# Four transformer layers on one core: inputs in pieces, and another order at four places

## What is computed

```python
x = inputs                                             # (1, 2048, 128)
x = layernorm(x + attention(x, Wq, Wk, Wv, Wo, ...))   # 16 heads of 8, all keys
x = layernorm(x + rope_attention_and_top2_experts(x))  # causal, 16 heads; then 2 of 8 experts
x = layernorm(x + mamba2_block(x))                     # conv, state-space scan, then a gated MLP of 344
x = layernorm(x + experts16(x))                        # sigmoid scores, 8 of 16 experts, and a shared one

def experts16(x):
    scores = sigmoid(x @ gate.T); inds = top8(scores + bias)
    combine = onehot(inds) * 2.826 * scores[inds] / sum(scores[inds])
    y = sum_e combine[e] * (silu(x @ w_gate[e].T) * (x @ w_up[e].T)) @ w_down[e].T
    return y + (silu(x @ sg.T) * (x @ su.T)) @ sd.T
```

## Time and profile before

| | us |
|---|---|
| median of 3 runs | 1793.71 (1791.2 to 1806.1) |
| the profiled execution | 1793.51 |
| its span | 1791.7 |
| mean granted clock of PE | 0.97 |

### The profile page before, as it was taken

One profiled execution on the slowest core, in us unless ns is written; L12 is line 12 of the kernel. 1 busy time (PEld: TensorE's weight loads), 2 busy tenths in 40 slices (PEclk: granted clock), 3 DMA queues, 4 the chain that ended last, 5 costly groups with the idle time before them and its releaser, 6 DMA issues. The chain is left out here.

```text
span 1791.7 us, 25880 instructions
## 1 busy us (share of the span) xinstructions
PE 1662.0 (93%) x9970; PEld 781.1 (44%) x9970; DVE 1271.6 (71%) x1818; ACT 1192.6 (67%) x2434; POOL 199.3 (11%) x187
## 2 busy tenths in 40 slices
PE   6999999999999999879899999999878599799997
PEld 3433333333333333244344444455555266444443
DVE  4888888888888888257888677675376376555555
ACT  4578888888888888855677777777635656233432
POOL 1100000000000000041000000111244100001100
PEclk9899999999999999989999999999989799899999
DMA  1000000000000000010000000000000100302220
...
DMA packets 8330, 29.98 MB, mean 17 GB/s; under 512 B 712, under 2 KB 3152, under 8 KB 6032
## 3 DMA queue, kind: packets, MB, share of 16 engines
...
## 5 line engine op out<-in xcount | busy, mean ns | idle before, releaser
L911 DVE TENSOR_REDUCE a_part_max<-a_ps 128x2 f32<-128x1024 f32 x512 | 602.8, 1221 | 90.8 <-PE a_ps L714 90.2
L896 ACT ACTIVATE a_probs<-a_ps 128x512 f32<-128x512 f32 x1024 | 533.0, 613 | 131.0 <-PE a_ps L809 128.6
L911 DVE TENSOR_REDUCE f_part_max<-f_ps 128x2 f32<-128x1024 f32 (+3 forms) x320 | 328.2, 1062 | 127.4 <-PE f_ps L714 67.2
L809 PE MATMUL a_ps<-a_q_shift,a_KA 64*128 64x512 f32 x1024 | 367.4, 447 | 3.8 <-POOL a_q_shift L693 2.4
L896 ACT ACTIVATE f_probs<-f_ps 128x512 f32<-128x512 f32 (+3 forms) x640 | 300.3, 538 | 101.0 <-PE f_ps L809 49.2
L809 PEld LDWEIGHTS a_ps<-a_q_shift,a_KA 64*128 64x128 f32 x1024 | 166.4, 186 | 290.2 <-ACT a_probs L896 274.9
L714 PE MATMUL a_ps<-a_KA,a_q_open 64*128 64x512 f32 x1024 | 276.5, 467 | 4.9 <-DVE a_part_max L911 4.2
L829 PE MATMUL a_psO<-a_probs,a_VA 128*32 128x512 f32 x2048 | 274.7, 608 | 3.9 <-ACT a_probs L896 3.9
L809 PE MATMUL f_ps<-f_q_shift,f_KA 64*128 64x512 f32 (+3 forms) x640 | 223.4, 434 | 5.2 <-POOL f_q_shift L693 2.2
L714 PE MATMUL f_ps<-f_KA,f_q_open 64*128 64x512 f32 (+3 forms) x640 | 168.7, 427 | 7.1 <-DVE f_part_max L911 6.3
L809 PEld LDWEIGHTS f_ps<-f_q_shift,f_KA 64*128 64x128 f32 x640 | 105.8, 187 | 149.7 <-ACT f_probs L896 138.8
...
## 6 DMA issues: line engine op xcount, KB each, us to landing
...
```

The lines of the kernel that those rows point to most:

```text
L809: mm = pe.matmul(bank(r)[:, lo:512], g.KA[rows, 2 * n + jp, P * s:P * s + P], q_shift[rows, u % 2, jp, lo:512], start=True, stop=not diag)
L896: nc.scalar.activation(probs[:, st % 2, j, lo:512], bank(r)[:, lo:512], ACT.Exp, scale=SCALE).then_inc(ring_read, 1)
L911: dve.tensor_reduce(part_max[:, 4 * q + 2 * jp:4 * q + 2 * jp + 2, c], ps1[:, k % 2, :, 0:b - a], AX_X, ALU.max).then_inc(max_read, 1)
```

## The change

- `load_stage` is gone. The first attention's `front_stage` gets a `Loads` object and issues ten transfers in its own program: x in four blocks, the identity apart from the other constants, and the weights for q and k apart from the others. Each wait is for its own piece. The casts and fills come at the end of the front's ScalarE list, the three bf16 casts behind a wait for the last pieces.
- In the first step of both attentions, PE has scores 0, 1 and 2 ahead of the maxima of the first half.
- In the scan, `gate_up`, `gated`, `project_down`, `add_mlp` and `mean` stand earlier.
- In the experts, the shared expert's `products` of block 0 stand ahead of `turn_c`.
- The last block's scaling: two tiles on ScalarE, two on DVE.

```diff
+class Loads:
+    def __init__(self, g):
+        self.x = [g.sem("x_in%d" % b) for b in range(NB)]
+        self.ident, self.first, self.cols, self.rest = (g.sem("loaded_" + x) for x in ("ident", "first", "cols", "rest"))
+    def issue(self, sp, g):
+        aps = g.aps
+        tokens = aps["x"].rearrange("(t p) e -> p t e", p=P)
+        a, b = W_COLS["wq"][0], W_COLS["wk"][1]
+        def x_block(n):
+            sp.dma_start(g.X[:, 4 * n:4 * n + 4, :], tokens[:, 4 * n:4 * n + 4, :]).then_inc(self.x[n], 16)
+        x_block(0)
+        sp.dma_start(g.K[:, 0:P], aps["consts"][:, 0:P]).then_inc(self.ident, 16)
+        sp.dma_start(g.W[:, a:b], aps["weights"][:, a:b]).then_inc(self.first, 16)
+        x_block(1)
+        sp.dma_start(g.C[:], aps["cols"]).then_inc(self.cols, 16)
+        x_block(2)
+        x_block(3)
+        sp.dma_start(g.K[:, P:K_N], aps["consts"][:, P:K_N]).then_inc(self.rest, 16)
+        sp.dma_start(g.R[:], aps["rows"].partition_broadcast(P)).then_inc(self.rest, 16)
+        sp.dma_start(g.W[:, b:W_LATER], aps["weights"][:, b:W_LATER]).then_inc(self.rest, 16)
+        sp.wait_ge(self.rest, 48)
...
+                if loads:
+                    loads.issue(sp, g)
...
+                if loads:
+                    pool.memset(g.half[:], -0.5).then_inc(half_in, 1)
+                    pool.memset(g.q_spread[:].bitcast(F32), 0.0).then_inc(sel_clear, 1)
                 pool.memset(g.k_spread[:].bitcast(F32), 0.0).then_inc(sel_clear, 1)
                 pool.memset(g.VA[:], 1.0).then_inc(v_ones, 1)
...
+                    if loads:
+                        pe.wait_ge(loads.x[b], 16)
+                        if b == 0:
+                            pe.wait_ge(loads.ident, 16)
...
+                    if loads:
+                        pe.wait_ge(loads.first, 16)
                     pe.matmul(bank, g.w(wk if kind == "k" else wq), source[:, cols(b)], start=True, stop=True).then_inc(qk_ps, 1)
...
+                    if loads:
+                        act.wait_ge(loads.cols, 16)
...
-                    act.wait_ge(sel_clear, 1)
+                    act.wait_ge(sel_clear, 2)
+                    fill_spread(g, g.q_spread, Q_PARTS, sel_in)
                     fill_spread(g, g.k_spread, K_PARTS, sel_in)
+                    nc.scalar.copy(g.ident_r[:], g.k("ident")).then_inc(sel_in, 1)
+                    act.wait_ge(loads.rest, 48)
+                    for name, dst in (("ident_h", g.ident_h), ("mask_qk_h", g.mask_qk), ("mask_kq_h", g.mask_kq)):
+                        nc.scalar.copy(dst[:].rearrange("p h i -> p (h i)"), g.k(name)).then_inc(sel_in, 1)
...
                 more(plan.before)
                 for st in range(plan.first[-1]):
                     scores(st, 0)
-                    more(plan.halves[2 * st])
+                    if st:
+                        more(plan.halves[2 * st])
                     scores(st, 1)
                     scores(st, 2)
+                    if st == 0:
+                        more(plan.halves[0])
                     if st:
                         sums(st - 1)
                     scores(st, 3)
...
                     n = b + 1
                     for i in range(4):
                         c = 4 * b + i
+                        if c == 13:
+                            t.gate_up(pe, 0, 1, ring(0), ring(1))
...
                         if c == 12:
                             pe.wait_ge(ring_read, ITEMS * NB)
-                        if 12 <= c < 15:
-                            t.gate_up(pe, 0, c - 12, ring(0), ring(1))
+                            t.gate_up(pe, 0, 0, ring(0), ring(1))
                         outputs(c)
+                        if c == 13:
+                            t.gate_up(pe, 0, 2, ring(0), ring(1))
+                        if c == 14:
+                            t.project_down(pe, 0, ring(0))
...
-                t.project_down(pe, 0, ring(0))
...
                         if c + 1 < C:
                             carry_on(c)
+                        if c == 14:
+                            t.gated(dve, 0, 2, ring(1))
+                        if c == 15:
+                            t.add_mlp(dve, 0, ring(0), eps)
...
                         if c == 11:
                             t.scale(dve, 0)
-                        if c >= 13:
-                            t.gated(dve, 0, c - 13, ring(1))
+                        if c in (12, 13):
+                            t.gated(dve, 0, c - 12, ring(1))
+                        if c == 15:
+                            t.mean(dve, 0)
...
                 finish(C - 1)
-                t.add_mlp(dve, 0, ring(0), eps)
-                t.mean(dve, 0)
...
                 turn_x(0)
                 route(0)
+                products(0, 0)
                 turn_c(0)
                 for b in range(NB):
                     c = b + 1
                     for x in range(NX + 1):
-                        if x < NX:
+                        if x < NX and (b or x):
                             products(b, x)
...
                 def apply_out(b):
                     act.wait_ge(nb2, b + 1)
-                    apply_norm(nc, blk(g.X, b), blk(g.Y, b), rstd[:, 1, b, :], nb[:, 1, b, :], sent)
+                    n = 2 if b == NB - 1 else 4
+                    for i in range(4 * b, 4 * b + n):
+                        nc.scalar.activation(g.X[:, i, :], g.Y[:, i, :], ACT.Identity, scale=rstd[:, 1, b, i % 4:i % 4 + 1],
+                                             bias=nb[:, 1, b, i % 4:i % 4 + 1]).then_inc(sent, 1)
...
                 mean_out(NB - 1)
+                dve.wait_ge(nb2, NB)
+                for i in (2, 3):
+                    at = 4 * (NB - 1) + i
+                    dve.tensor_scalar(g.X[:, at, :], g.Y[:, at, :], rstd[:, 1, NB - 1, i:i + 1], nb[:, 1, NB - 1, i:i + 1],
+                                      ALU.mult, ALU.add).then_inc(sent, 1)
```

40 lines of the change are left out of this document (9 added, 31 removed).

## The result

The changed kernel took 1783.62 us (median of 20 runs, 1777.0 to 1793.99) against 1793.35 us of the kernel before (20 runs, 1788.56 to 1806.65): the ratio is 0.994, with a 95% interval of 0.9923 to 0.9957, so between 7.7 and 13.8 us less. The profiled execution was one of 1784.2 us, with a span of 1782.4 (before 1791.7). The 20 times of the changed kernel lie in three groups: seven from 1777.0 to 1779.7, seven from 1782.4 to 1784.4 and six from 1790.1 to 1794.0.

What follows compares the result with a forecast made beforehand. TensorE, busy 93% of the span, was taken as the bound, with time to be had only where it waits or runs slowly. Five local terms, 6.2 + 0.6 + 4.3 + 0.7 + 0.8 = 12.6 us off 1793.5, gave 1781 us, range 1774 to 1788.

Steps and rivals of the forecast that it cites:

- Loads in pieces: Kernel start: smaller transfers let the attention start 7.0 us earlier; less 0.8 for a slower clock, 6.2 us (3 to 8).
- the charge of 0.8 us for the clock: Start: 0.8 us deducted because TensorE, idle about 4 us before the first attention, would begin it more slowly.
- a stretch that was at full clock falls to half: Anywhere in the kernel: one of three stated signs that would show the prediction wrong; no size given.
- rival C: Start: issuing ten transfers costs so much that the kernel gets slower, 1797 us at 3 us per issue; chance 0.03.
- First steps: First step of both attentions: three score blocks ahead of the maxima save 0.3 us each, 0.6 us together.
- Scan: Scan's end: two waits for VectorE's product vanish and the down projection moves ahead of chunk 15's outputs: 4.3 us (2.5 to 5).
- The 0.2 for finish(14): Scan's end: finish(14) on VectorE is covered by GpSimd's power except for 0.2 us, charged against the gain.
- First experts: First experts' stage: product ahead of the coefficients' turn, then bound by the coefficients' transfer: 0.7 us (-0.3 to 2.5).
- Rival A: Start, attentions' first steps and first experts: the clock stays up, 17.9 us saved in all, 1775.6 us; chance 0.14.
- Last scaling: Kernel's end: two of four ScalarE scalings move to VectorE beside them, saving 0.8 us (0.6 to 0.9).

Runs made afterwards that it cites:

- first_step_only: The kernel before with only the new order of TensorE's work in both attentions' first step: 1792.51 us (ten runs), ratio 0.9991.

## Why the prediction was right, and where a term was off

Forecast 1781 us, range 1774 to 1788, and a chance of 0.86 for a change of under 1%: measured 1783.6 and 0.6% less. The five mechanisms are those that the text named, and the sum of 12.6 us lies in the measured 7.7 to 13.8. How near the number came is in part luck. Two traces of the changed kernel are 9.3 and 14.5 us shorter than that of the kernel before, the forecast lies between, and none of the 20 executions took between 1779.7 and 1782.4 us. In the profiled pair the pieces add up: 3.53 us at the first a_neg_max, -0.15 in the first step, -1.45 from there to the second attention's first maximum, 0.41 in its first step, 0.13 to the scan's end, 4.81 there, 1.24 in the first experts and 0.78 behind them, 9.3 in all. Term by term:

- **Loads in pieces: 6.2 forecast.** The start itself: in five traces with the old loads the attention starts at 24.21 to 25.74 (mean 25.02), in four with the new ones and nothing else done to the stage at 17.27 to 18.34 (mean 17.79): 7.2, forecast 7.0. The inside of it was less exact. The first transposes came at 3.91, not 5.0: the quarter and the identity were there at 3.9, 3.2 us after the first issue. The second quarter was late by 1.07 us where I had called the waits short, and ScalarE's tail ended at 17.75 against 18.4. The text took the fill at 24.02 for the end of the stage before; it was VectorE's split, 0.5 us behind the fill, but with the casts moved ScalarE's tail is the longer one, as forecast. Errors of a microsecond stood against each other. The step that failed is the charge of 0.8 us for the clock, a term too small. It cost 4.15 us more than before in the profiled execution, and over the same traces the stretch to a_neg_max took 44.77 us on the mean against 43.04: 1.7 us. So the term is 5.5 us on the mean, 3.5 in the profiled execution. The text said that "a stretch that was at full clock falls to half" would make it wrong; from 17.4 to 31.1 us that is what happened there.
- **Issuing, rival C.** Each of the ten issues held the queue 0.42 to 0.51 us (the first is in the rows of the start above), far under the 2.00 us of the earlier trace rows and the 2.7 at which the gain would be gone. What made the 2.00 stays open: the text puts it down to the transfer with the shortest rows, but C's rows are shorter (15 KB over 128 partitions), and the issue behind C took 0.43 us. The rule of the Trainium skill, "DMA: Bandwidth & Descriptors", Bandwidth / Measured, that speaks for transfers of 1 MiB and more (the fixed 2 us that the prediction names with it stand on the same page under Anatomy of one DMA) did not decide here: in this kernel latency until the first piece counts, and the last transfer, noticed at 12.26 in the kernel with the casts on GpSimd (11.42 before the change), may come a little later, since in the changed kernel nobody waits for it.
- **First steps: 0.6 forecast,** 0.45 measured on the mean (0.14 in the first attention without the two traces that stand apart, 0.31 in the second). The first is half of what was forecast.
- **Scan: 4.3 forecast,** 4.8 measured, in every trace with the whole edit. No up matmul waits for VectorE any more. The products gave 2.25 where I had 2.3. The down projection gave 2.55 where I had 2.2 less 0.2. The 0.2 for finish(14) was not needed: with it on VectorE, the row behind GpSimd's power still came 0.06 us after that (1537.71 against 1536.63 and 1.02). And chunk 15's outputs take 2.56 us with their waits, where I had 2.2.
- **First experts: 0.7 forecast,** 0.67 measured with that edit alone at the matmul that was named, through the bound that was named (the transfer). From the first transpose to t_var, five traces with both edits show 48.18 to 48.86 us (mean 48.41), four with neither 48.99 to 49.43 (one of these has the scan's products; mean 49.21): 0.8 us on the mean, 1.24 in the profiled execution. Rival A had put the clock's gain there at 2.5 us; it came to about half a microsecond in some executions and to nearly nothing in others, and with TensorE filled to 1.5 or a little more.
- **Last scaling: 0.8 forecast,** 0.77 measured (1.67 to 0.90 us).

Terms as measured on the mean: 5.5 + 0.45 + 4.8 + 0.8 + 0.8 = 12.3 us. The medians say 9.7, with an interval that holds both. What the rulers leave out can make a difference of that size; how much of it is whose isn't shown. There are stretches of half clock elsewhere: one at 768 cost 1.6 us, and one of 3.4 us near 1410 was there in seven of the fourteen traces, those of before and of the change among them, and those without it were 2.5 us faster there. And there are the executions some 10 us above the others, 6 of 20 for the changed kernel and 4 of 20 before (19 of 86 over all measurements of the kernel before). Whether the change makes those more frequent can't be told.

The period near 1410 is no mere accident of the clock. There GpSimd starts a product (L1786 in the kernel before) when a transfer of 512 KB, mx_z, has landed, and TensorE waits for the product. In the seven traces with the period the product starts 4.60 to 4.88 us behind the transfer's issue, in the seven without it 3.80 to 4.10, and from TensorE's first matmul on the product to its next transposes it is 8.64 us with the period and 6.95 without. So of the 2.5 us some 0.8 are the transfer and 1.7 the slower clock. The late product comes first (1409.22 in the kernel before, the half clock from 1412.6), and TensorE waits 2.15 us for it there, 1.35 in first_step_only, which has no such period. Why the transfer is late in half of the traces stays open.
